# Two softmax products of an attention loop moved from VectorE to GpSimd, and the gate stage's scratch buffers halved

## The chip, the cores and the metric

The kernel runs as one program on all 8 NeuronCores of one Trainium2 chip, without any exchange between the cores. Each core works on half of one of four sequences. The metric is the device time of the slowest core in microseconds (us). Each core has five engines that run side by side and meet only in semaphores: TensorE (PE in the profile), VectorE (DVE), ScalarE (ACT), GpSimd (POOL) and SyncE (SP). DMAs are issued from the queues of SP, ACT and POOL.

## The reference

A layer of gated attention with bounded memory slots (ABC), then a mixture of low-rank maps, each added to its input and put through a layer norm. What matters here is the softmax in the middle of the attention and the gate behind it:

```python
z = cumlogsumexp(s); g = exp(z_prev - z); p = exp(s - z)
hk = hk * g_t + k_t * p_t;   ok = einsum('bhk,bhkm->bhm', q_t, hk)
pv = softmax(ok)                      # over M = 64 slots
hv = hv * g_t + p_t * v_t;   ov = einsum('bhm,bhmv->bhv', pv_t, hv)
g = x @ Wg
o = ov * rsqrt(mean(ov**2) + EPS) * g_norm_weight
o = o * (g * sigmoid(g));    x = layernorm(x + o @ Wo)
...                                    # mixture of 8 low-rank maps, second layer norm
```

There are 16 heads of 64 (keys, slots) and 128 (values), a model width of 2048 and 2048 positions in a sequence.

## The kernel before

A core first runs over 1024 positions that lie ahead of its own to get the recurrent states. Then it handles its own 1024 positions in two halves of 512, each of 4 chunks of 128 positions (NHC = 4). A half consists of stages: projections S, K, V and Q, the attention loop, the gate stage, the output product with Wo, a layer norm, and the mixture.

**The attention loop.** One turn is a chunk and a group of 4 heads (GH = 4), so a half has NIT = 16 turns, and the kernel has 32. The turns are pipelined by hand in the order of this loop, and every engine executes its own instructions in that order:

```python
for it in range(NIT + 1):
    if it < NIT:
        p_front(it)
    if 0 <= it - 1 < NIT:
        p_back(it - 1)
    if it < NIT:
        p_np(it)
        p_pv(it)
```

- `p_front` transposes keys, queries and e = exp(s) on TensorE; ScalarE copies them to `kqfm` and `efm`; TensorE multiplies them into FB[0], ScalarE copies this to `arw`, and GpSimd applies the causal mask (`abf`).
- `p_np` adds up numerator and denominator in a PSUM bank, FB[2] or FB[3].
- `p_pv` turns these into the weights. ScalarE makes `rbuf` = 1/denominator as exp(-ln), VectorE `okb` = numerator times `rbuf`, ScalarE `ebuf` = exp(`okb`); VectorE then sums `ebuf` per head into `sm4` (shown as sm), takes the reciprocal, multiplies `ebuf` by `rbuf` in place, and multiplies that by `sm4` into the bf16 tile `cbf`.
- `p_back` transposes `cbf` on TensorE (bank TBK[1], shown as tb); ScalarE copies it to `cfm`; TensorE multiplies with `efm` into FB[4], ScalarE copies this to `wrw`, GpSimd masks it (`wbf`), and TensorE makes the output and the update of the states, which VectorE adds to `s1f`, `psf` and `s2f` (each in float32).

**The gate stage** has two passes (vh = 0, 1) for the halves of the value columns. A pass first squares the 4 chunks of the attention's output `ovh` on ScalarE into a scratch tile `obs`, sums each on VectorE into `msq`, and takes square root and reciprocal once for all four. Then, for each chunk c: `g_proj(c)` multiplies with Wg on TensorE (32 products of 128x512), `g_evac(c)` copies the result on VectorE into `gsc`, and `g_gate(c)` takes Silu of it on ScalarE into `sgs`, multiplies `ovh` by `msq` and then by the norm weight on GpSimd into `obs`, multiplies `obs` by `sgs` on VectorE into the bf16 tile `otb`, and transposes `otb` on TensorE into `ofm`. TensorE's order in a pass is g_proj(0), g_proj(1), transposes of chunk 0, g_proj(2), transposes of chunk 1, and so on. `obs`, `sgs` and `otb` exist twice each, one for even and one for odd chunks. A pass ends in a barrier before the next begins.

**Waits.** A helper records each operation. On VectorE and ScalarE, and for operations recorded by `gop` on GpSimd, each instruction waits for its own engine's semaphore as well (the previous instruction's completion) besides the waits it names. Each wait is an instruction of its own (line 53), and `P.wait` leaves a wait out when that engine has already waited for the same or a later count of that semaphore:

```python
if n <= 0 or self.hw[eng].get(sem, 0) >= n:
    return
```

SBUF is handed out by a small allocator (`Arena`), which gives a new buffer the tokens of what was freed there to wait for.

Of the kernel before, what the change touches and what calls it, by code (L numbers as in the profile page):

```python
# [8 lines left out]
F32 = mybir.dt.float32  # L9
BF16 = mybir.dt.bfloat16  # L10
# [152 lines left out]
def build_program(cfg):  # L163
# [37 lines left out]
    with ctx:  # L201
# [65 lines left out]
        def vop(fn, waits=()):  # L267
            P.waits("vector", waits)
            P.wait("vector", ("VE", P.sems["VE"].n))
            return P.inc("vector", "VE", _eager(fn))  # L270

        def sop(fn, waits=()):
            P.waits("scalar", waits)
            P.wait("scalar", ("SC", P.sems["SC"].n))
            return P.inc("scalar", "SC", _eager(fn))
# [365 lines left out]
        for half in range(2):  # L641
# [155 lines left out]
            tok_cC = [None] * NIT  # L797
            tok_tc = [None] * NIT
            ex_prev = [None]

            def scp(out_ap, in_ap, waits=()):
                return sop(lambda s, o=out_ap, i=in_ap: s.copy(o, i), waits=waits)
# [86 lines left out]
            def p_pv(it):  # L889
                NPB = FB[2] if it % 2 == 0 else FB[3]  # L890
                cbf = cbfb[it % 2]
                lnp = sop(lambda s: s.activation(
                    rbuf.ap(0, 128, 0, GH * M), NPB[0:128, GH * M:2 * GH * M],
                    AF.Ln, bias=0.0, scale=1.0),
                    waits=[tok_mtN[it]] + rbuf.birth)
                vop(lambda v: v.memset(rbuf.h[0:1, 0:1], 0)) if False else None
                sop(lambda s: s.activation(
                    rbuf.ap(0, 128, 0, GH * M), rbuf.ap(0, 128, 0, GH * M),
                    AF.Exp, bias=0.0, scale=-1.0), waits=[lnp])
                ok = vop(lambda v: v.tensor_tensor(  # L900
                    okb.ap(0, 128, 0, GH * M), NPB[0:128, 0:GH * M],
                    rbuf.ap(0, 128, 0, GH * M), ALU.mult),
                    waits=[ex_prev[0], P.cur("SC")] + okb.birth)
                bset(NPB, ok)
                ex = sop(lambda s: s.activation(
                    ebuf.ap(0, 128, 0, GH * M), okb.ap(0, 128, 0, GH * M),
                    AF.Exp, bias=0.0, scale=1.0),
                    waits=[P.cur("VE")] + ebuf.birth)
                ex_prev[0] = ex
                vop(lambda v: v.tensor_reduce(  # L910
                    sm4.ap(0, 128, 0, GH),
                    ebuf.ap3(0, 128, 0, [[M, GH], [1, M]]), AX.X, ALU.add),
                    waits=[ex] + sm4.birth)
                vop(lambda v: v.reciprocal(sm4.ap(0, 128, 0, GH),
                                           sm4.ap(0, 128, 0, GH)))
                vop(lambda v: v.tensor_tensor(
                    ebuf.ap(0, 128, 0, GH * M), ebuf.ap(0, 128, 0, GH * M),
                    rbuf.ap(0, 128, 0, GH * M), ALU.mult))
                tok_cC[it] = vop(lambda v, cb=cbf: v.tensor_tensor(
                    cb.ap(0, 128, 0, GH * M), ebuf.ap(0, 128, 0, GH * M),  # L920
                    sm4.ap3(0, 128, 0, [[1, GH], [0, M]]), ALU.mult),
                    waits=([tok_tc[it - 2]] if it >= 2 else []) + cbf.birth)

            def p_back(it):
                c, g = divmod(it, NG)
# [135 lines left out]
            ofm = AR.alloc("ofm", [128, VDC * TH], BF16)  # L1061
            gsc2 = [AR.alloc("gsc", [128, GV], F32) for _ in range(2)]
            gsc2_free = [None, None]
            sgs2 = [AR.alloc("sgs", [128, GV], F32) for _ in range(2)]
            obs2 = [AR.alloc("obs", [128, GV], F32) for _ in range(2)]
            otb2 = [AR.alloc("otb", [128, GV], BF16) for _ in range(2)]
            otb_free2 = [None, None]
            sgs_free2 = [None, None]
            obs_free2 = [None, None]
            msq = AR.alloc("msq", [128, NHC * HH], F32)  # L1070
            ofm_tok = [None] * NHC
            wg_pre[1] = load_w("wgb2", wg, D, VD, col0=GV, ncols=GV)
# [1 line left out]
            for vh in range(2):  # L1074
                if vh == 1:
                    wo_pre[0] = load_w("wob2", wo, VD, D, col0=0, ncols=D2)
                wgb2, twg2 = wg_pre[vh]
                sq = None
                for c in range(NHC):
                    obs = obs2[c % 2]  # L1080
                    sq = sop(lambda s, c=c, vh=vh, obs=obs: s.activation(
                        obs.ap(0, 128, 0, GV),
                        ov_ap(c, vh * GV, GV), AF.Square,
                        bias=0.0, scale=1.0),
                        waits=bPAT + [obs_free2[c % 2]] + obs.birth)
                    obs_free2[c % 2] = vop(
                        lambda v, c=c, obs=obs: v.tensor_reduce(
                            msq.ap(0, 128, c * HH, HH),
                            obs.ap3(0, 128, 0, [[DV, HH], [1, DV]]),
                            AX.X, ALU.add),  # L1090
                        waits=[sq] + msq.birth)
                si = sop(lambda s: s.activation(msq.ap(0, 128, 0, NHC * HH),
                                                msq.ap(0, 128, 0, NHC * HH),
# [37 lines left out]

                def g_gate(c, vh):
                    gsc = gsc2[c % 2]
                    sgs = sgs2[c % 2]
                    obs = obs2[c % 2]
                    otb = otb2[c % 2]
                    sg = None
                    for g in range((GV + 511) // 512):
                        cn = min(512, GV - g * 512)
                        sg = sop(lambda s, g=g, cn=cn, sgs=sgs, gsc=gsc:  # L1140
                                 s.activation(
                            sgs.ap(0, 128, g * 512, cn),
                            gsc.ap(0, 128, g * 512, cn),
                            AF.Silu, bias=0.0, scale=1.0),
                            waits=[gv_tok[c][g], sgs_free2[c % 2]] + sgs.birth)
                    gsc2_free[c % 2] = sg
                    gop(lambda g, c=c, vh=vh, obs=obs: g.tensor_tensor(
                        obs.ap(0, 128, 0, GV),
                        ov_ap(c, vh * GV, GV),
                        msq.ap3(0, 128, c * HH, [[1, HH], [0, DV]]),  # L1150
                        ALU.mult), waits=[iv, obs_free2[c % 2]] + obs.birth)
                    o2 = gop(lambda g, obs=obs: g.tensor_tensor(
                        obs.ap(0, 128, 0, GV), obs.ap(0, 128, 0, GV),
                        gnw_sb.ap3(0, 128, 0, [[0, HH], [1, DV]]),
                        ALU.mult), waits=[t_gnw])
                    o3 = vop(lambda v, obs=obs, sgs=sgs, otb=otb:
                             v.tensor_tensor(
                        otb.ap(0, 128, 0, GV), obs.ap(0, 128, 0, GV),
                        sgs.ap(0, 128, 0, GV), ALU.mult),
                        waits=[sg, o2, otb_free2[c % 2]] + otb.birth)  # L1160
                    sgs_free2[c % 2] = o3
                    obs_free2[c % 2] = o3
                    for j0 in range(0, HH, 4):
                        nj = min(4, HH - j0)
                        bnk = TBK[j0 // 4 % 2]
                        mt = None
                        for j in range(nj):
                            mt = mm(bnk[0:128, j * 128:(j + 1) * 128],
                                    otb.ap(0, 128, (j0 + j) * DV, DV),
                                    idb_sb.h[0:128, 0:128],  # L1170
                                    start=(j == 0), stop=(j == nj - 1),
                                    waits=[o3, t_idb, bfree(bnk)] if j == 0 else (),
                                    inc=(j == nj - 1), tp=True)
                        evt = vop(lambda v, b=bnk, nj=nj, c=c, j0=j0, vh=vh:
                                  v.tensor_copy(
                                      ofm.ap3(0, 128,
                                              (vh * HH + j0) * TH + c * 128,
                                              [[TH, nj], [1, 128]]),
                                      b[0:128, 0:nj * 128]),
                                  waits=[mt] + ofm.birth)  # L1180
                        bset(bnk, evt)
                        ofm_tok[c] = evt
                    return P.cur("MM")

                for c in range(NHC + 1):
                    if c < NHC:
                        g_proj(c)
                    if c - 1 >= 0:
                        otb_free2[(c - 1) % 2] = g_gate(c - 1, vh)
                    if c < NHC:  # L1190
                        g_evac(c)
                bPAT = phase_barrier()
                AR.freebuf(wgb2, toks=bPAT)
                AR.freebuf(ovhh[vh], toks=bPAT)

            for b in (msq, otb2[0], otb2[1], obs2[0], obs2[1], sgs2[0],
                      sgs2[1], gsc2[0], gsc2[1]):
                AR.freebuf(b, toks=bPAT)
            AR.freebuf(xmf, toks=bPAT)

# [462 lines left out]
```

How the kernel before makes its waits and increments, by code:

```python
    def wait(self, eng, tok):  # L43
        if tok is None:
            return
        sem, n = tok
        if sem in self.ONESHOT and n > 0:
            n = self.sems[sem].n
        if n <= 0 or self.hw[eng].get(sem, 0) >= n:
            return
        self.hw[eng][sem] = n
        h = self.sems[sem].h
        self.streams[eng].append(lambda e, h=h, n=n: e.wait_ge(h, n))
        self.ninst[eng] += 1
# [9 lines left out]
    def inc(self, eng, sem, fn, dn=1):  # L64
        s = self.sems[sem]
        s.n += dn
        h = s.h
        self.streams[eng].append(lambda e, fn=fn, h=h, dn=dn: fn(e).then_inc(h, dn))
        self.ninst[eng] += 1
        return (sem, s.n)
```

## Time and profile before

| what | us |
|---|---|
| median of 3 runs (1890.65 to 1899.34) | 1892.87 |
| the profiled execution: its own time | 1893.43 |
| the profiled execution: span of its slowest core (core 5) | 1891.9 |
| spans of the 8 cores | 1876.2 to 1891.9 |
| TensorE busy on core 5 | 1306.0 |
| VectorE busy | 544.5 |
| ScalarE busy | 412.6 |
| GpSimd busy | 234.4 |

The profile is one execution, read on its slowest core; times in it are counted from the first instruction. The own time of the execution is 1.5 us more than the span. The attention loops lie at about 576 to 786 and 1324 to 1534, the gate stages at about 787 to 866 and 1535 to 1614. PE rows show matrix products, whose overlap lets their mean duration exceed their spacing; some of their records can be missing. Idle time in square brackets ahead of an instruction is followed by what ended it.

### The profile page before, as it was taken

Reading aid. Unit: us, or ns where it says so; the run is one execution under the profiler, and the core shown is the slowest. Engines: PE = TensorE matmul, PEld = TensorE weight load, DVE = VectorE, ACT = ScalarE, POOL = GpSimd, SP = SyncE. Lnnn points to the kernel's source line nnn. Section 1 sums busy time; section 2 is a strip of 40 time slices with the busy share of each in tenths; the row PEclk is TensorE's granted clock in tenths of the full one; section 3 lists DMA queues with packets and bytes.
Section 4 is the critical chain, followed back from the end, with each engine's and each line's share of the span. In section 5 each row is a group of like instructions: output and inputs, shape, how many; then the busy total and the mean of one; then the engine's idle time right before and its main releaser. Section 6 shows DMA issues by size and latency. Waiting matters only on the chain.

```text
span 1891.9 us, 18782 instructions; the slowest of 8 cores (1876.2 to 1891.9 us)
## 1 busy us (share of the span) xinstructions
PE 1306.0 (69%) x6800; PEld 643.1 (34%) x6800; DVE 544.5 (29%) x886; ACT 412.6 (22%) x568; POOL 234.4 (12%) x220
## 2 busy tenths in 40 slices
PE   2449898978995554588585757979555568758662
PEld 0114444434443333344242323424333334324231
DVE  2012323242001222354431272000222245352145
ACT  0000000001113444421110122102444432120013
POOL 2100000000002111251100001100211145110000
PEclk9769999988995555689887768979555579979776
DMA  9950010002405000277975149980500046893502
GB/s 175 178 97 23 26 42 23 23 25 81 73 1 90 1 1 1 42 113 156 219 117 89 16 74 225 172 137 1 90 1 1 1 78 101 172 179 72 89 1 89
DMA packets 61515, 146.25 MB, mean 77 GB/s; under 512 B 7536, under 2 KB 12016, under 8 KB 56048
## 3 DMA queue, kind: packets, MB, share of 16 engines
q0 software_dynamic: 54800, 102.90, 35.1%
q1 hardware_dynamic: 5472, 33.76, 5.4%
q10 hardware_dynamic: 1152, 8.39, 1.1%
q8 instruction: 55, 0.90, 0.2%
q14 instruction: 36, 0.29, 0.1%
HBM read 237.45 MB, written 8.39 MB: 130 GB/s over the span
## 4 chain that ended last, share of the span: by engine, by line
PE 47%; DMA 18%; DVE 15%; ACT 8%; issue 6%; POOL 4%; DVEq 1%; ACTq 0%; POOLq 0%
PE fb L245 45%; DMA wvb<-wv 6%; DMA wob<-wo 4%; DMA wkb<-wk 3%; DMA w1b<-w 3%; PE tb L245 2%; POOL wbf L265 2%; DMA wsb<-ws 1%; ACT rbuf L265 1%; DVE x1bufs L265 1%; DVE msq L265 1%; DVE st L265 1%; ACT wrw L265 1%; ACT cfm L265 1%; DVE sm L265 1%
## 5 line engine op out<-in xcount | busy, mean ns | idle before, releaser
L245 PE MATMUL fb<-w1b,x2fm 128*128 128x512 bf16 x512 | 130.5, 417 | 34.5 <-DMA w1b<-w 34.5
L245 PE MATMUL fb<-wvb,xpf 128*128 128x512 bf16 x512 | 119.1, 393 | 31.8 <-DMA wvb<-wv 31.8
L245 PE MATMUL fb<-wob,ofm 128*128 128x512 bf16 x512 | 118.0, 394 | 19.4 <-DMA wob<-wo 19.4
L245 PE MATMUL fb<-wvb,xmf 128*128 128x512 bf16 x512 | 117.2, 392 | 13.9 <-DMA wvb<-wv 13.9
L245 PE MATMUL fb<-wgb,xmf 128*128 128x512 bf16 x512 | 122.0, 401 | 0.0
L265 DVE TENSOR_TENSOR okb<-fb,rbuf 128x256 f32<-128x256 f32 x32 | 13.6, 424 | 310.2 <-ACT rbuf L265 168.9
L245 PE MATMUL fb<-wsb,xpf 128*128 128x512 bf16 x256 | 70.0, 435 | 32.8 <-DMA wsb<-ws 19.5
L245 PEld LDWEIGHTS fb<-w1b,x2fm 128*128 128x128 bf16 x512 | 52.1, 104 | 105.4 <-issue 57.0
L265 DVE TENSOR_TENSOR s1f<-s1f,fb 64x256 f32<-64x256 f32 (+1 forms) x48 | 24.1, 502 | 209.0 <-PE fb L245 207.3
L245 PEld LDWEIGHTS fb<-wvb,xpf 128*128 128x128 bf16 x512 | 50.6, 100 | 97.5 <-issue 42.8
L245 PEld LDWEIGHTS fb<-wob,ofm 128*128 128x128 bf16 x512 | 51.4, 101 | 85.3 <-issue 30.0
L245 PE MATMUL fb<-idf,strip 128*128 128x128 f32 x256 | 42.1, 302 | 55.1 <-DVE xmf L265 28.2
L245 PEld LDWEIGHTS fb<-wvb,xmf 128*128 128x128 bf16 x512 | 50.9, 100 | 79.9 <-issue 23.0
L245 PE MATMUL fb<-wsb,xmf 128*128 128x512 bf16 x256 | 68.6, 435 | 8.5 <-DVE xmf L265 8.5
L245 PEld LDWEIGHTS fb<-wgb,xmf 128*128 128x128 bf16 x512 | 52.1, 103 | 64.9 <-issue 12.4
L245 PE MATMUL fb<-wkb,xpf 128*128 128x512 bf16 x256 | 62.0, 398 | 14.2 <-DMA wkb<-wk 14.2
L265 POOL TENSOR_TENSOR abf<-arw,lmb 128x512 bf16<-128x512 bf16 x32 | 36.8, 1151 | 273.7 <-ACT arw L265 273.7
L265 ACT ACTIVATE scrf<-x1bufs 128x1024 f32<-128x1024 f32 (+1 forms) x24 | 32.2, 1342 | 163.8 <-DVE x1bufs L265 163.8
L245 PE MATMUL fb<-utb,vxwf 128*128 128x512 bf16 x128 | 50.7, 583 | 24.0 <-DVE x1bufs L265 21.5
L265 ACT ACTIVATE scrb<-scrf 128x1024 bf16<-128x1024 f32 x16 | 16.9, 1057 | 230.3 <-DVE scrf L265 230.3
L265 ACT ACTIVATE echk<-fb,pb 128x512 bf16<-128x512 f32 x16 | 11.0, 688 | 251.9 <-DVE fb L265 251.9
L265 DVE TENSOR_SCALAR fb<-fb 128x512 f32<-128x512 f32 x32 | 22.4, 699 | 142.6 <-PE fb L245 141.8
(149 smaller groups left out, 1897.7 us busy)
## 6 DMA issues: line engine op xcount, KB each, us to landing
strip<-x_main SPq DMA_DIRECT2D x24, 1024.0 KB, 10.1
wvb<-wv POOLq DMA_DIRECT2D x16, 1024.0 KB, 34.7
wgb<-wg POOLq DMA_DIRECT2D x16, 1024.0 KB, 19.6
wob<-wo POOLq DMA_DIRECT2D x16, 1024.0 KB, 21.2
w1b<-w POOLq DMA_DIRECT2D x16, 1024.0 KB, 23.6
strip<-x_pre SPq DMA_DIRECT2D x8, 1024.0 KB, 8.2
wqb<-wq POOLq DMA_DIRECT2D x8, 1024.0 KB, 32.0
y<-x1bufs ACTq DMA_DIRECT2D x8, 1024.0 KB, 4.8
```

What stands on the lines that cost most here:

```text
L245: t.matmul(o, l, r, start=a, stop=b, is_transpose=(True if tpp else None)))
L265: return lambda e, n=name, a=a, k=k: getattr(e, n)(*a, **k)
```

## The change

In `p_pv`, the product of `ebuf` with `rbuf` and the product into `cbf` are recorded for GpSimd in place of VectorE. The first waits for the exponential, for the second activation into `rbuf` and for the sum `sm`; the second for the reciprocal. New waits guard the buffers: the logarithm into `rbuf` waits for the previous turn's first product, and the exponential into `ebuf` and the sum into `sm4` wait for the previous turn's second product. In the gate stage, `obs`, `sgs` and `otb` exist once each in place of twice, with the waits that this asks for.

```diff
                 lnp = sop(lambda s: s.activation(
                     rbuf.ap(0, 128, 0, GH * M), NPB[0:128, GH * M:2 * GH * M],
                     AF.Ln, bias=0.0, scale=1.0),
-                    waits=[tok_mtN[it]] + rbuf.birth)
-                vop(lambda v: v.memset(rbuf.h[0:1, 0:1], 0)) if False else None
-                sop(lambda s: s.activation(
+                    waits=[tok_mtN[it], e2_prev[0]] + rbuf.birth)
+                rex = sop(lambda s: s.activation(
...
                 ex = sop(lambda s: s.activation(
                     ebuf.ap(0, 128, 0, GH * M), okb.ap(0, 128, 0, GH * M),
                     AF.Exp, bias=0.0, scale=1.0),
-                    waits=[P.cur("VE")] + ebuf.birth)
+                    waits=[P.cur("VE"), cC_prev[0]] + ebuf.birth)
                 ex_prev[0] = ex
-                vop(lambda v: v.tensor_reduce(
+                sm = vop(lambda v: v.tensor_reduce(
                     sm4.ap(0, 128, 0, GH),
                     ebuf.ap3(0, 128, 0, [[M, GH], [1, M]]), AX.X, ALU.add),
-                    waits=[ex] + sm4.birth)
-                vop(lambda v: v.reciprocal(sm4.ap(0, 128, 0, GH),
-                                           sm4.ap(0, 128, 0, GH)))
-                vop(lambda v: v.tensor_tensor(
+                    waits=[ex, cC_prev[0]] + sm4.birth)
+                rc = vop(lambda v: v.reciprocal(sm4.ap(0, 128, 0, GH),
+                                                sm4.ap(0, 128, 0, GH)))
+                e2_prev[0] = gop(lambda g: g.tensor_tensor(
                     ebuf.ap(0, 128, 0, GH * M), ebuf.ap(0, 128, 0, GH * M),
-                    rbuf.ap(0, 128, 0, GH * M), ALU.mult))
-                tok_cC[it] = vop(lambda v, cb=cbf: v.tensor_tensor(
+                    rbuf.ap(0, 128, 0, GH * M), ALU.mult),
+                    waits=[ex, rex, sm])
+                tok_cC[it] = gop(lambda g, cb=cbf: g.tensor_tensor(
                     cb.ap(0, 128, 0, GH * M), ebuf.ap(0, 128, 0, GH * M),
                     sm4.ap3(0, 128, 0, [[1, GH], [0, M]]), ALU.mult),
-                    waits=([tok_tc[it - 2]] if it >= 2 else []) + cbf.birth)
+                    waits=[rc] + ([tok_tc[it - 2]] if it >= 2 else [])
+                    + cbf.birth)
+                cC_prev[0] = tok_cC[it]
...
-            sgs2 = [AR.alloc("sgs", [128, GV], F32) for _ in range(2)]
-            obs2 = [AR.alloc("obs", [128, GV], F32) for _ in range(2)]
-            otb2 = [AR.alloc("otb", [128, GV], BF16) for _ in range(2)]
-            otb_free2 = [None, None]
-            sgs_free2 = [None, None]
-            obs_free2 = [None, None]
+            sgs = AR.alloc("sgs", [128, GV], F32)
+            obs = AR.alloc("obs", [128, GV], F32)
+            otb = AR.alloc("otb", [128, GV], BF16)
+            otb_free = None
+            sgs_free = [None]
...
-                        waits=bPAT + [obs_free2[c % 2]] + obs.birth)
+                        waits=bPAT + [obs_free] + obs.birth)
...
-                        ALU.mult), waits=[iv, obs_free2[c % 2]] + obs.birth)
+                        ALU.mult), waits=[iv, sgs_free[0]] + obs.birth)
...
-                        waits=[sg, o2, otb_free2[c % 2]] + otb.birth)
-                    sgs_free2[c % 2] = o3
-                    obs_free2[c % 2] = o3
+                        waits=[sg, o2, otb_free] + otb.birth)
+                    sgs_free[0] = o3
```

## Rows read from the trace of the kernel before

**Rows 1.** The page's head: its span.
```profile
span 1891.9 us, 18782 instructions; the slowest of 8 cores (1876.2 to 1891.9 us)
```

**Rows 2.** Windows: stretch, length, busy us (instructions) of PE, PEld, DVE, ACT, POOL, PEclk, DMA, GB/s.
```profile
586.00:786.00 200.00, 105.05 (x781) 71.12 (x780) 52.08 (x123) 90.81 (x145) 34.44 (x30) 0.51 0.09 15
...
860.00:865.00 5.00, 0.38 (x5) 0.41 (x6) 3.14 (x5) 1.26 (x2) 0.00 (x0) 0.70 0.00 0
```

**Rows 3.** Timeline of one turn of the attention loop: start us, busy us, instruction.
```profile
643.79 0.39 ACT L265 ACTIVATE rbuf<-fb 128x256 f32<-128x256 f32 x1 [1.94 <-PE fb L245]
...
644.27 0.42 ACT L265 ACTIVATE rbuf<-rbuf 128x256 f32<-128x256 f32 x1
...
644.86 0.42 DVE L265 TENSOR_TENSOR okb<-fb,rbuf 128x256 f32<-128x256 f32 x1 [0.63 <-ACT rbuf L265]
645.43 0.42 ACT L265 ACTIVATE ebuf<-okb 128x256 f32<-128x256 f32 x1 [0.74 <-DVE okb L265]
...
646.02 0.42 DVE L265 TENSOR_REDUCE sm<-ebuf 128x4 f32<-128x256 f32 x1 [0.74 <-ACT ebuf L265]
646.54 0.18 DVE L265 RECIPROCAL sm<-sm 128x4 f32<-128x4 f32 x1
646.82 0.42 DVE L265 TENSOR_TENSOR ebuf<-ebuf,rbuf 128x256 f32<-128x256 f32 x1
...
647.35 0.42 DVE L265 TENSOR_TENSOR cbf<-ebuf,sm 128x256 bf16<-128x256 f32 x1
647.81 0.59 ACT L265 CAST arw<-fb 128x512 bf16<-128x512 f32 x1 [0.20 <-PE fb L245]
...
648.03 0.60 PE L245 MATMUL tb<-idb,cbf 128*64 128x128 bf16 x4 [0.36 <-DVE cbf L265]
648.54 1.15 POOL L265 TENSOR_TENSOR abf<-arw,lmb 128x512 bf16<-128x512 bf16 x1 [8.15 <-ACT arw L265]
648.78 0.58 ACT L265 COPY cfm<-tb 64x512 bf16<-64x512 bf16 x1 [0.38 <-PE tb L245]
...
649.50 0.58 PE L245 MATMUL fb<-cfm,efm 64*128 64x128 bf16 x4 [0.87 <-ACT cfm L265]
```

**Rows 4.** Timeline of the gate stage's first pass, half 0, other engines than TensorE.
```profile
788.83 5.19 DVE L265 TENSOR_REDUCE msq<-obs 128x8 f32<-128x1024 f32 x4 [4.62 <-ACT obs L265]
790.20 1.06 ACT L265 ACTIVATE obs<-ovh 128x1024 f32<-128x1024 f32 x1 [0.46 <-DVE msq L265]
...
796.34 1.89 POOL L265 TENSOR_TENSOR obs<-ovh,msq 128x1024 f32<-128x1024 f32 x1 [5.26 <-DVE msq L265]
...
798.38 2.34 POOL L265 TENSOR_TENSOR obs<-obs,gnw 128x1024 f32<-128x1024 f32 x1
...
800.86 1.89 POOL L265 TENSOR_TENSOR obs<-ovh,msq 128x1024 f32<-128x1024 f32 x1
800.89 2.95 DVE L265 TENSOR_TENSOR otb<-obs,sgs 128x1024 bf16<-128x1024 f32 x1 [3.11 <-POOL obs L265]
...
808.30 3.35 DVE L265 TENSOR_TENSOR otb<-obs,sgs 128x1024 bf16<-128x1024 f32 x1 [1.02 <-POOL obs L265]
811.86 1.90 POOL L265 TENSOR_TENSOR obs<-ovh,msq 128x1024 f32<-128x1024 f32 x1 [1.29 <-DVE otb L265]
...
817.10 1.23 DVE L265 TENSOR_TENSOR otb<-obs,sgs 128x1024 bf16<-128x1024 f32 x1 [1.02 <-ACT sgs L265]
```

**Rows 5.** Timeline of TensorE after chunk 0's gate, first and second pass.
```profile
803.98 1.01 PE L245 MATMUL tb<-idb,otb 128*128 128x128 bf16 x8 [7.33 <-DVE otb L265]
...
804.79 8.35 PE L245 MATMUL fb<-wgb,xmf 128*128 128x512 bf16 x32
...
844.42 0.61 PE L245 MATMUL tb<-idb,otb 128*128 128x128 bf16 x8 [1.38 <-DVE otb L265]
...
844.87 7.07 PE L245 MATMUL fb<-wgb,xmf 128*128 128x512 bf16 x32
```

**Rows 6.** Groups by line of GpSimd, whole span: count, busy us, mean ns.
```profile
L182 POOL MEMSET const-float32-0.0<- 128x1 f32 x1 | 0.1, 98 | 0.5 <-issue 0.5
```

More of the change, by code:

```diff
@@ L799, in build_program @@
             ex_prev = [None]
+            e2_prev = [None]
+            cC_prev = [None]
             def scp(out_ap, in_ap, waits=()):
@@ L1078, in build_program @@
                 sq = None
+                obs_free = None
                 for c in range(NHC):
-                    obs = obs2[c % 2]
-                    sq = sop(lambda s, c=c, vh=vh, obs=obs: s.activation(
+                    sq = sop(lambda s, c=c, vh=vh: s.activation(
                         obs.ap(0, 128, 0, GV),
@@ L1084, in build_program @@
                         bias=0.0, scale=1.0),
-                        waits=bPAT + [obs_free2[c % 2]] + obs.birth)
[L1086 to L1090, printed above, removed]
+                        waits=bPAT + [obs_free] + obs.birth)
+                    obs_free = vop(lambda v, c=c: v.tensor_reduce(
+                        msq.ap(0, 128, c * HH, HH),
+                        obs.ap3(0, 128, 0, [[DV, HH], [1, DV]]), AX.X, ALU.add),
                         waits=[sq] + msq.birth)
@@ L1133, in g_gate @@
                     gsc = gsc2[c % 2]
-                    sgs = sgs2[c % 2]
-                    obs = obs2[c % 2]
-                    otb = otb2[c % 2]
                     sg = None
@@ L1139, in g_gate @@
                         cn = min(512, GV - g * 512)
-                        sg = sop(lambda s, g=g, cn=cn, sgs=sgs, gsc=gsc:
-                                 s.activation(
+                        sg = sop(lambda s, g=g, cn=cn: s.activation(
                             sgs.ap(0, 128, g * 512, cn),
@@ L1144, in g_gate @@
                             AF.Silu, bias=0.0, scale=1.0),
-                            waits=[gv_tok[c][g], sgs_free2[c % 2]] + sgs.birth)
+                            waits=[gv_tok[c][g], sgs_free[0]] + sgs.birth)
                     gsc2_free[c % 2] = sg
-                    gop(lambda g, c=c, vh=vh, obs=obs: g.tensor_tensor(
+                    gop(lambda g, c=c, vh=vh: g.tensor_tensor(
                         obs.ap(0, 128, 0, GV),
@@ L1150, in g_gate @@
                         msq.ap3(0, 128, c * HH, [[1, HH], [0, DV]]),
-                        ALU.mult), waits=[iv, obs_free2[c % 2]] + obs.birth)
-                    o2 = gop(lambda g, obs=obs: g.tensor_tensor(
+                        ALU.mult), waits=[iv, sgs_free[0]] + obs.birth)
+                    o2 = gop(lambda g: g.tensor_tensor(
                         obs.ap(0, 128, 0, GV), obs.ap(0, 128, 0, GV),
@@ L1155, in g_gate @@
                         ALU.mult), waits=[t_gnw])
-                    o3 = vop(lambda v, obs=obs, sgs=sgs, otb=otb:
-                             v.tensor_tensor(
+                    o3 = vop(lambda v: v.tensor_tensor(
                         otb.ap(0, 128, 0, GV), obs.ap(0, 128, 0, GV),
                         sgs.ap(0, 128, 0, GV), ALU.mult),
-                        waits=[sg, o2, otb_free2[c % 2]] + otb.birth)
-                    sgs_free2[c % 2] = o3
-                    obs_free2[c % 2] = o3
+                        waits=[sg, o2, otb_free] + otb.birth)
+                    sgs_free[0] = o3
                     for j0 in range(0, HH, 4):
@@ L1188, in build_program @@
                     if c - 1 >= 0:
-                        otb_free2[(c - 1) % 2] = g_gate(c - 1, vh)
+                        otb_free = g_gate(c - 1, vh)
                     if c < NHC:
@@ L1194, in build_program @@
                 AR.freebuf(ovhh[vh], toks=bPAT)
-            for b in (msq, otb2[0], otb2[1], obs2[0], obs2[1], sgs2[0],
-                      sgs2[1], gsc2[0], gsc2[1]):
+            for b in (msq, otb, obs, sgs, gsc2[0], gsc2[1]):
                 AR.freebuf(b, toks=bPAT)
```

## The prediction

> **What bounds the kernel now.** I read the page's head first [rows 1], then the chain of work that ended last, then a timeline of one turn of the attention loop [rows 3] and of a pass of the gate stage [rows 4, 5], and at the end windows over the stages [rows 2]. No engine is the bound where the change lands. In the 200 us of the attention loop no engine is busy for more than 105 us, and the DMA engines do nothing much (0.09) [rows 2]. The reader is to see in [rows 3] that the loop is one serial thread: each instruction of it begins 0.1 to 0.3 us after the one before it ends, on another engine or the same. Numerator and denominator, logarithm, exponential, `okb`, `ebuf`, sum, reciprocal, product, product, transposes of `cbf`, copy to `cfm`, product into FB[4], mask, output, and then TensorE goes on to the next turn's numerator, which stands behind all this in its queue. So every 0.1 us added to this thread is paid 32 times. In the gate stage the reader is to see that TensorE stands idle before the first transposes of each pass (7.33 and 1.38 us) and that this idle time ends with `otb` of chunk 0 [rows 5]. From the squares to `otb` of chunk 0 it is one thread too. After it TensorE runs g_proj(2) and g_proj(3) and is the thread itself.
>
> **Waits, priced.** Each wait is an instruction, so the gap ahead of an operation tells its price. On ScalarE the gap with one wait is 644.27 - 644.18 = 0.09 us and with two 645.43 - 645.28 = 0.15: 0.06 for a wait. On VectorE 0.10 with one (646.54 - 646.44) and 0.17 with two (646.02 - 645.85): 0.07. On TensorE 0.14 with one (649.50 - 649.36) and 0.26 with two (648.03 - 647.77): 0.12 [rows 3]. On GpSimd 0.15 with one (798.38 - 798.23) and 0.21 with two, after VectorE (811.86 - 811.65) [rows 4].
>
> **Attention loop, what goes and what comes.** From the end of the sum (646.44) to the start of the transposes (648.03) it is 1.59 us now: gap 0.10, reciprocal 0.18, gap 0.10, product 0.42, gap 0.11, product 0.42, gap 0.26 [rows 3]. After the change the first product needs the sum but not the reciprocal, which runs beside it on VectorE at no cost (0.10 + 0.18 us after the sum; its cover is the GpSimd product, over 0.5 us long). If that cover fails, it costs at most what is left of the 0.28 us. The new thread is: gap to GpSimd with two waits 0.21, first product, gap 0.15, second product, gap to TensorE 0.26.
>
> The trace has no GpSimd product of 256 elements. The nearest are two of 1024 float32 elements, 2.34 us with two plain operands and 1.89 with one operand repeated along the row [rows 4], and the mask of 512 bf16 elements, 1.15 [rows 3]. By size alone the first product (two plain operands) is 2.34/4 = 0.585 and the second (`sm4` repeated along the row, like `msq`) 1.89/4 = 0.47. That is the low end, as size alone leaves no fixed part. A fixed part is bounded by the memset of one column, 0.10 [rows 6]: 0.10 + 2.24/4 = 0.66 for either is the high end, as the second may not have the faster rate with bf16 out and rows of 64. The far bound, 1.15 each, is that of twice the elements and is left out, since 2.34 against 1.15 shows time going with size. I take 0.64 and 0.56, nearer the high end, since some fixed part is likely. The new stretch is 0.21 + 0.64 + 0.15 + 0.56 + 0.26 = 1.82, which is 0.23 more than 1.59.
>
> By the Trainium skill (GPSIMD Engine Reference, section Elementwise, side-by-side cycle accounting) a two-input product of 2048 float32 elements takes 4497 ns on GpSimd. An estimate from that page's figure and the trace's 2.34 us for 1024 makes the fixed part 0.19 and a product of 256 elements 0.73 us; with 0.73 for both the stretch would be 0.49 longer than now in place of 0.23, and the total below about 8 us higher. No row here shows 2048 elements.
>
> **Waits that are added on the thread.** The logarithm waits for the previous first product and the exponential into `ebuf` for the previous second one. Both are long done, but each is an instruction behind a wait that resolves late: 2 x 0.06 on ScalarE. The sum waits for it too: 0.07 on VectorE. A fourth is not in the diff. TensorE used to wait on VectorE's semaphore for `cbf`, and this covered the wait of the product into FB[4] for its bank (freed by VectorE's `s2f` addition). Now `cbf` is counted by GpSimd's semaphore, so `P.wait` no longer drops the bank's wait: 0.12 on TensorE between `cfm` and that product. Together 0.31 a turn. Queued behind them are only the instructions of the same thread. The mask `abf` of the next turn now stands behind the second product on GpSimd. That product ends at about 646.51 + 0.21 + 0.64 + 0.15 + 0.56 = 648.07 on the old turn's clock, while `abf` can't start before 648.54, when `arw` is copied [rows 3], so it isn't delayed; above 0.5 us more it would be.
>
> Sum for the loop: 0.23 + 0.31 = 0.54 a turn, x 32 = 17.3 us. With the low products (0.585, 0.47) it is 0.39 and 12.6 us, with the high ones (0.66, 0.66) 0.66 and 21 us. If the added waits cost nothing because they are taken off ahead of time, the low end is 0.085 a turn, 2.7 us. TensorE's granted clock is 0.51 in the loop, its level of 1.2 GHz [rows 2]; it can't fall further through longer gaps.
>
> **Gate stage, squares.** With two `obs` tiles the four sums into `msq` follow each other: 788.83 + 5.19 = 794.02 is the end [rows 4]. With one, square c+1 waits for sum c. Square 1.06, gap 0.17, sum 1.22, gap 0.15 (790.20 - 790.05 [rows 4]) make a period of 2.60. The first sum ends at 790.05, the fourth at 790.05 + 3 x 2.60 = 797.85: 3.8 us later. All of it lies on the thread to `otb` of chunk 0 (`msq`, two GpSimd products, `otb`).
>
> **Gate stage, what comes back.** `otb` of chunk 0 takes 2.95 us, that of chunk 2, when GpSimd is idle, 1.23. GpSimd begins chunk 1's product at 800.86, 0.03 before `otb` at 800.89; 1.86 of waiting and 1.09 of work make 2.95 [rows 4]. With one `obs`, GpSimd's chunk 1 waits for `otb` of chunk 0, so the two can't meet: 1.72 us less. Net 3.8 - 1.7 = 2.1 us later for the first transposes of a pass, in 4 passes: 8.4 us. The rule behind this is in the Trainium skill (SBUF, section Who interferes with whom): a VectorE instruction with two SBUF inputs and a GpSimd instruction that reads SBUF hold a shared port pair one at a time. The trace agrees (2.95 against 1.23). The same rule lets the reciprocal and the reduction pass beside GpSimd, as assumed above; no row here shows that.
>
> The rest of a pass stays hidden. Chunk 1 on GpSimd now begins after `otb` of chunk 0 and takes 0.21 + 1.89 + 0.15 + 2.34, then `otb` 0.2 + 1.23, 6.0 us in all; TensorE is busy for at least 7.07 with g_proj(2) before it asks for it [rows 5]. Should it take 1 us more than I think, nothing happens yet. Chunks 2 and 3 have the same period and as much room.
>
> TensorE's idle time in second passes grows from 1.38 to about 3.5 us. After 1.38 us the next 32 products took 7.07; after 7.33 they took 8.35 and the transposes 0.4 more [rows 5]. So the price is between 0 and 1.7 us in each of two second passes. I take 0.8 each, 1.6 together. First passes pay this already.
>
> Nothing swallows the delay: between the gate stage and the load of the second half of Wo, which the output product waits for, the DMA engines stand idle (0.00 [rows 2]), so that load is issued later by what the gate stage is late. The allocator puts all weight buffers where they were, worked through on paper with the smaller set, so no load gets other tokens.
>
> **Sum.** 17.3 + 8.4 + 1.6 = 27.3 us on the profiled execution's 1893.43 (span 1891.9 and 1.5 around it [rows 1]), which is 0.6 above the median of 1892.87. I forecast 1920. What a measurement of this kernel can tell from no change is about 0.5%, 9.5 us.
>
> **The rivals.**
> - *Only size counts and waits are free.* The wait instructions resolve early and GpSimd has no fixed part: 2.7 + 8.4 = 11 us, 1904. For it: the waits' tokens are old. Against: they stand behind late ones in the same queue. Chance 0.12; together with a smaller gate loss part of it falls within 0.5%.
> - *GpSimd's small products are dear.* Fixed part of 0.2 us or more (the estimate above), or rows of 64 slow: 0.8 each, a stretch 0.63 longer, 0.94 a turn with the waits, 30 us + 10 = 40, 1933. For it: no row of a short product. Chance 0.17.
> - *The squares hide and the loop's waits hide* while the GpSimd products cost by size: 2.7 less 4 x 1.72, 1889, or 12.6 less the same if only the squares hide, 1899; no measurable change. Against it: the idle time before the first transposes ends with `otb`, in both passes. Chance 0.06.
> - *Unblocking wins.* If what TensorE waits for were `otb` in every chunk, and the squares were hidden, lifting the blocking would give back 1.72 in a first chunk and 3.35 - 1.23 = 2.12 in the next, 3.8 a pass, 15 us in 4 passes, and with the loop at its low end of 2.7 us 1881: faster. It decides from the point where `otb` of chunk 1 ends after g_proj(2). Against it: 808.30 + 3.35 = 811.65 lies before 804.79 + 8.35 = 813.14 [rows 4, 5]. Chance 0.03.
> - *As forecast*: 0.62.
>
> Range 1905 to 1932: the lower end takes in most of the first rival, the upper the high products, the full clock price and part of the second. Slower by over 0.5%: 0.87; within 0.5%: 0.10; faster: 0.03.
>
> **What would show it.** A turn's stretch from `sm` to the transposes of 1.8 us (1.6 now), GpSimd products of 0.64 and 0.56, a gap of about 0.26 ahead of FB[4]'s product, turns 0.5 us longer; sums into `msq` 2.6 us apart; all `otb` at 1.23; TensorE idle 2 us longer before a pass's first transposes; the second passes' first 32 products between 7.1 and 8.4 us. The prediction is wrong if GpSimd products are far from 0.6, or if the four added waits don't show in the gaps.

## The result and the profile after

The changed kernel takes 1928.0 us (median of 9 runs; the kernel before, run beside it, 1896.4 over 10): a ratio of 1.0167, 95% interval 1.0151 to 1.0183, or some 31.6 us more. Some executions of the runs below were disturbed, and the ratios leave them out. The forecast was 1920 in a range of 1905 to 1932.

From the page of the changed kernel:

```profile
span 1924.4 us, 19006 instructions; the slowest of 8 cores (1910.9 to 1924.4 us)
...
PE 1312.9 (68%) x6800; PEld 645.8 (34%) x6800; DVE 505.1 (26%) x822; ACT 412.5 (21%) x568; POOL 271.9 (14%) x284
```

VectorE has 64 instructions fewer and GpSimd 64 more; VectorE's busy time falls by 39 us (the moved products, and otb rows that no longer stand blocked). None of that shortens anything, as no engine was the bound.

One turn of the loop in the changed kernel, timeline, against [rows 3]:

```profile
647.69 0.42 DVE L265 TENSOR_TENSOR okb<-fb,rbuf 128x256 f32<-128x256 f32 x1 [0.68 <-ACT rbuf L265]
648.32 0.42 ACT L265 ACTIVATE ebuf<-okb 128x256 f32<-128x256 f32 x1 [0.80 <-DVE okb L265]
...
648.98 0.42 DVE L265 TENSOR_REDUCE sm<-ebuf 128x4 f32<-128x256 f32 x1 [0.86 <-ACT ebuf L265]
649.50 0.18 DVE L265 RECIPROCAL sm<-sm 128x4 f32<-128x4 f32 x1
649.60 0.72 POOL L265 TENSOR_TENSOR ebuf<-ebuf,rbuf 128x256 f32<-128x256 f32 x1 [6.43 <-DVE sm L265]
...
650.47 0.61 POOL L265 TENSOR_TENSOR cbf<-ebuf,sm 128x256 bf16<-128x256 f32 x1
...
651.34 0.61 PE L245 MATMUL tb<-idb,cbf 128*64 128x128 bf16 x4 [0.78 <-ACT arw L265]
...
652.09 0.58 ACT L265 COPY cfm<-tb 64x512 bf16<-64x512 bf16 x1 [0.80 <-PE tb L245]
...
652.92 0.58 PE L245 MATMUL fb<-cfm,efm 64*128 64x128 bf16 x4 [0.98 <-ACT cfm L265]
...
658.98 0.39 ACT L265 ACTIVATE rbuf<-fb 128x256 f32<-128x256 f32 x1 [2.00 <-PE fb L245]
...
660.68 0.42 ACT L265 ACTIVATE ebuf<-okb 128x256 f32<-128x256 f32 x1 [0.80 <-DVE okb L265]
```

The reader is to see the products at 0.72 and 0.61 us, 1.94 us from the end of the sum (649.40) to the transposes (651.34) where it was 1.59, and four gaps that have grown: 0.21 ahead of the exponential (0.15 before), 0.24 ahead of the sum (0.17), 0.25 ahead of the product into FB[4] (0.14), and the one ahead of the logarithm, 0.06 more by the idle time in its row (2.00 for 1.94). A turn takes 660.68 - 648.32 = 12.36 us. The releaser named in one row misleads: the transposes' row names `arw`, where [rows 3] name `cbf`, but they begin 0.26 us after `cbf` ends at 651.08, the same gap as before.

The first pass of the gate stage, half 0, timeline (VectorE and GpSimd), against [rows 4]:

```profile
801.17 1.22 DVE L265 TENSOR_REDUCE msq<-obs 128x8 f32<-128x1024 f32 x1 [1.38 <-ACT obs L265]
...
803.76 1.22 DVE L265 TENSOR_REDUCE msq<-obs 128x8 f32<-128x1024 f32 x1 [1.38 <-ACT obs L265]
...
806.36 1.22 DVE L265 TENSOR_REDUCE msq<-obs 128x8 f32<-128x1024 f32 x1 [1.38 <-ACT obs L265]
...
814.46 1.22 DVE L265 TENSOR_TENSOR otb<-obs,sgs 128x1024 bf16<-128x1024 f32 x1 [3.11 <-POOL obs L265]
...
815.89 1.90 POOL L265 TENSOR_TENSOR obs<-ovh,msq 128x1024 f32<-128x1024 f32 x1 [1.60 <-DVE otb L265]
```

The sums stand 2.6 us apart, `otb` takes 1.22, and GpSimd waits for it. TensorE after chunk 0's gate, timeline, first pass and second, against [rows 5]:

```profile
815.83 1.01 PE L245 MATMUL tb<-idb,otb 128*128 128x128 bf16 x8 [8.88 <-DVE otb L265]
...
816.64 9.38 PE L245 MATMUL fb<-wgb,xmf 128*128 128x512 bf16 x32
...
859.10 1.01 PE L245 MATMUL tb<-idb,otb 128*128 128x128 bf16 x8 [4.49 <-DVE otb L265]
...
859.90 8.23 PE L245 MATMUL fb<-wgb,xmf 128*128 128x512 bf16 x32
```

The first 32 products after the gap take 9.38 and 8.23 us where they took 8.35 and 7.07.

This table is worked out from such rows. "Turn" is the spacing of the rows of `ebuf` on ScalarE. "Loop" is from the first of them to the end of the last copy to `psb`, in half 0 of the slowest core. "Gate" runs from there to the end of the last transposes of `otb`, both halves added, as the mean of the 8 cores.

| kernel | turn | loop, one half | gate, both halves |
|---|---|---|---|
| before | 11.73 | 206.2 | 156.5 |
| changed | 12.35 | 215.6 | 169.3 |
| e1, loop only | 12.36 | 215.7 | 159.7 |
| e2, gate only | 11.72 | 206.1 | 171.8 |
| e3, waits early | 12.06 | 210.9 | 168.1 |
| e4, scratch tiles for squares | 12.35 | 215.6 | 157.7 |
| e5, filled gap | 12.35 | 215.7 | 165.0 |
| e6, product beside the sum | 11.44 | 200.9 | 162.7 |
| e7, scratch, loop of before | 11.72 | 206.1 | 158.8 |
| e8, e6 and e7 | 11.44 | 200.9 | 152.0 |
| e9, before again | 11.72 | 206.1 | 160.6 |
| e10, changed again | 12.35 | 215.6 | 172.6 |
| e11, as e7 | 11.73 | 206.1 | 153.2 |

The loop is 9.5 us longer in half 0 and 10.0 in half 1, and the gate 12.8, together 32.3. The spans of the 8 cores grow by 32.7 us on average and the measured time by 31.6, so this is the whole loss.

Where the table differs between kernels with the same gate code (156.5 and 160.6 for the kernel before, 169.3 and 172.6 for the changed one, 156.5 and 159.7 for e1), it shows stretches of a lower granted clock, of which e9 to e11 tell. The ratios below are each against the kernel before in runs beside them, which had a median of 1904.8 us for e1 to e4 and of 1907.3 for e5 to e8, so a few us of difference between a ratio and the 1.0167 above are not to be read.

### The profile page after: what moved, and what is told of

It is laid out like the page before. It is cut to its first block, busy times and chain, and to the rows that moved or that the text cites. A ratio compares the mean times of both kernels' runs of the same rounds, so it can differ in the third digit from the quotient of the medians.

```text
span 1924.4 us, 19006 instructions; the slowest of 8 cores (1910.9 to 1924.4 us)
## 1 busy us (share of the span) xinstructions
PE 1312.9 (68%) x6800; PEld 645.8 (34%) x6800; DVE 505.1 (26%) x822; ACT 412.5 (21%) x568; POOL 271.9 (14%) x284
## 4 chain that ended last, share of the span: by engine, by line
PE 50%; DMA 15%; DVE 13%; ACT 10%; issue 6%; POOL 4%; DVEq 1%; ACTq 1%; POOLq 0%
PE fb L245 47%; DMA wvb<-wv 6%; DMA wob<-wo 4%; DMA w1b<-w 3%; PE tb L245 2%; POOL wbf L265 2%; ACT kqfm L265 1%; DMA wsb<-ws 1%; ACT rbuf L265 1%; DVE x1bufs L265 1%; DMA wkb<-wk 1%; DVE msq L265 1%; DVE st L265 1%; DVE xmf L265 1%; ACT wrw L265 1%
## 5 line engine op out<-in xcount | busy, mean ns | idle before, releaser
L245 PE MATMUL fb<-wgb,xmf 128*128 128x512 bf16 x512 | 126.3, 411 | 0.0
L245 PE MATMUL fb<-kqfm 64*128 64x128 bf16 x128 | 18.2, 292 | 68.1 <-ACT kqfm L265 68.1
L233 POOL DMA_DIRECT2D wqb<-wq x8 | 6.0, 760 | 395.7 <-ACT eh L265 395.7
```

The costliest lines, as they stand in the source:

```text
L233: lambda e, o=out_ap, i=in_ap: e.dma_start(out=o, in_=i), 16)
L245: t.matmul(o, l, r, start=a, stop=b, is_transpose=(True if tpp else None)))
```

## The experiments

**The two halves of the change.** e1 is the changed loop with the gate stage of before, e2 the changed gate stage with the loop of before.

> The loop's half of the change with the gate stage of before. Theory: a turn grows from 11.72 to 12.36 us (longer GpSimd products and four added waits), 32 x 0.64 = 20.5 us, so about 1.011 of before, and the gate stage stays as it was. Rival, that the gate stage carries most of the loss: under 12 us, below 1.007.

Measured: 1.0112 (1.0053 to 1.0171), a turn of 12.36.

> The gate stage's half of the change with the loop of before. Theory: 8.4 us from the serial squares less the lifted blocking, plus some 6 us of TensorE at its lower level after longer idle time, 14 us, 1.0075 of before. Rival, that the clock rows belong to something else in the changed loop: 8.4 us, 1.0045, and the second passes' first 32 products at 7.07.

Measured: 1.0057 (1.0023 to 1.0092), the loop untouched. The interval holds both the theory's 1.0075 and the rival's 1.0045, so the rows decide: behind the gap, the second passes of the slowest core ran their 32 products in 9.57 and 9.39 us, so these long rows don't need the changed loop. The two ratios add up to the whole.

**The price of the waits.** e3 puts three of the four added waits ahead of the wait that resolves late. The fourth, ahead of the exponential, goes: the logarithm now waits for the previous turn's second product in place of its first, and this covers it.

```diff
-                    waits=[tok_mtN[it], e2_prev[0]] + rbuf.birth)
+                    waits=[cC_prev[0], tok_mtN[it]] + rbuf.birth)
...
-                    waits=[P.cur("VE"), cC_prev[0]] + ebuf.birth)
+                    waits=[P.cur("VE")] + ebuf.birth)
...
-                    waits=[ex, cC_prev[0]] + sm4.birth)
+                    waits=[cC_prev[0], ex] + sm4.birth)
...
-                            waits=([tok_cC[it], t_idb, bfree(TBK[1])]
+                            waits=([bfree(FB[4]), tok_cC[it], t_idb, bfree(TBK[1])]
```

> The changed kernel with the four added waits of a turn put ahead of the wait that resolves late. Theory, each wait behind a late one costs its 0.06 to 0.12 us: a turn 12.36 - 0.30 = 12.06 us, about 9.6 us less than the changed kernel, 1.0115 of before. Rival, that waits on old tokens are free: turn 12.36, nothing gained.

Timeline of e3, ScalarE and TensorE:

```profile
646.56 0.42 ACT L265 ACTIVATE ebuf<-okb 128x256 f32<-128x256 f32 x1 [0.75 <-DVE okb L265]
...
650.25 0.58 ACT L265 COPY cfm<-tb 64x512 bf16<-64x512 bf16 x1 [0.72 <-PE tb L245]
650.97 0.58 PE L245 MATMUL fb<-cfm,efm 64*128 64x128 bf16 x4 [0.87 <-ACT cfm L265]
...
658.62 0.42 ACT L265 ACTIVATE ebuf<-okb 128x256 f32<-128x256 f32 x1 [0.75 <-DVE okb L265]
```

The gap ahead of FB[4]'s product is back at 0.14 us and the turn is 658.62 - 646.56 = 12.06, 0.30 less. The ratio is 1.0111 (1.0065 to 1.0157), the loop 2 x 4.7 us shorter. The waits were on old tokens and still cost 0.30 us a turn, for they were executed behind the late one. The rival, that they are free, is out. Of the 0.30, the 0.06 of the exponential were won by leaving its wait out and not by moving it.

**The gate without serial squares.** e4 gives the squares two scratch tiles of their own (`sqs2`) and leaves `obs`, `sgs` and `otb` single.

```diff
+            sqs2 = [AR.alloc("sqs", [128, GV], F32) for _ in range(2)]
...
-                    sq = sop(lambda s, c=c, vh=vh: s.activation(
-                        obs.ap(0, 128, 0, GV),
+                    sqs = sqs2[c % 2]
+                    sq = sop(lambda s, c=c, vh=vh, sqs=sqs: s.activation(
+                        sqs.ap(0, 128, 0, GV),
...
-                        waits=bPAT + [obs_free] + obs.birth)
+                        waits=bPAT + [sqs_free[c % 2]] + sqs.birth)
```

> The changed kernel with two scratch tiles of their own for the squares, while obs, sgs and otb stay single in the gate. Theory: sums 1.3 us apart again and otb of 1.23 us, so a pass is 1.7 us shorter than before and TensorE's idle time in second passes falls to nothing: the loop's 20.5 less 7, some 13.5 us over before, 1.007. Rival, that the single obs in the gate is what costs (GpSimd's next chunk waits for otb): still near 1.0167.

Measured: 1.0101 (1.0057 to 1.0145). The gate loses the change's loss (157.7 for 169.3), so single buffers in the gate itself are not what costs. It falls short of the 149.6 that the theory asks for (156.5 less 4 x 1.72). Many of its g_proj took 8.57 us (see e9 to e11), and the 32 products behind the first pass's gap took 9.4 us in half 0 on all cores, where they took 8.35 in the kernel before, although the gap was shorter (5.3 us for 7.3).

**The clock after idle time.** e5 adds products of no use to the changed kernel, ahead of chunk 0's transposes, where TensorE would stand idle.

```diff
+                    if c == 1:
+                        for i in range(32 if vh == 0 else 14):
+                            mm(FB[4][0:128, 0:512], xslc(0)(i % KC),
+                               wgb2.ap(0, 128, (i % KC) * GV, 512),
+                               start=True, stop=True,
+                               waits=[bfree(FB[4])] if i == 0 else ())
                     if c - 1 >= 0:
                         otb_free = g_gate(c - 1, vh)
```

> The changed kernel with added products of no use (32 in a first pass, 14 in a second, 128x512 into the bank FB[4] that this stage leaves free) ahead of chunk 0's transposes, where TensorE stands idle. Theory, TensorE falls to its lower level after long idle time: with the gap filled g_proj(2) takes 7.07 us in every pass and the transposes 0.61, some 9 us less than the changed kernel, 1.012 of before. Rival, that g_proj(2) is long for another reason (a bank or a port): it stays at 8.2 to 9.4.

Timeline of e5, TensorE of core 0, first and second pass of half 0:

```profile
813.83 0.61 PE L245 MATMUL tb<-idb,otb 128*128 128x128 bf16 x8 [1.96 <-DVE otb L265]
814.27 7.07 PE L245 MATMUL fb<-wgb,xmf 128*128 128x512 bf16 x32
...
854.43 0.61 PE L245 MATMUL tb<-idb,otb 128*128 128x128 bf16 x8
854.88 7.07 PE L245 MATMUL fb<-wgb,xmf 128*128 128x512 bf16 x32
```

Windows of the changed kernel (core 5) during and after the first 5 us behind the gap, and of e5 (core 0) in the same place:

```profile
816.00:820.00 4.00, 4.00 (x16) 1.85 (x15) 2.23 (x4) 1.26 (x2) 3.86 (x2) 0.50 1.09 170
822.00:826.00 4.00, 4.00 (x22) 1.88 (x21) 0.00 (x0) 0.00 (x0) 3.86 (x2) 1.00 1.08 195
```

```profile
814.00:822.00 8.00, 8.00 (x50) 4.05 (x48) 3.72 (x6) 1.26 (x2) 6.11 (x4) 1.00 1.08 179
```

Behind the gap the granted clock is 0.50 (1.2 GHz) and then 1.00 (2.4 GHz) in the changed kernel, and 1.00 throughout in e5. With the gap filled the 32 products take 7.07 us in both passes, and on six cores the two halves' gates take 80.5 and 80.9 us where the changed kernel's take 84.6 and 84.7 (means of the 8 cores), 8 us less. The ratio is 1.0090 (1.0052 to 1.0128). So the long rows were the granted clock after idle time. The kernel before pays for it too, in its first passes: from the start of chunk 0's transposes to the end of the next 32 products its four passes take 33.6 us together (mean of the 8 cores), where 4 x 7.51 is the time at full clock. That is 3.5 us, so without the clock its gate would be 153.0, and 153.0 + 8.4 for the later transposes is e5's 161.4. On cores 4 and 5 the halves took 90 and 85 us: on core 5 all g_proj of 32 products in half 0, and in the second pass of half 1, took 8.57; of these below.

**A use of GpSimd that pays.** e6 takes the kernel before and moves only the first product, into a tile of its own, so that it can start with the sum and not after it. The second stays on VectorE.

```diff
+                e2 = gop(lambda g: g.tensor_tensor(
+                    prbuf.ap(0, 128, 0, GH * M), ebuf.ap(0, 128, 0, GH * M),
+                    rbuf.ap(0, 128, 0, GH * M), ALU.mult),
+                    waits=[cC_prev[0], ex, rex] + prbuf.birth)
...
-                vop(lambda v: v.tensor_tensor(
-                    ebuf.ap(0, 128, 0, GH * M), ebuf.ap(0, 128, 0, GH * M),
-                    rbuf.ap(0, 128, 0, GH * M), ALU.mult))
                 tok_cC[it] = vop(lambda v, cb=cbf: v.tensor_tensor(
-                    cb.ap(0, 128, 0, GH * M), ebuf.ap(0, 128, 0, GH * M),
+                    cb.ap(0, 128, 0, GH * M), prbuf.ap(0, 128, 0, GH * M),
                     sm4.ap3(0, 128, 0, [[1, GH], [0, M]]), ALU.mult),
-                    waits=([tok_tc[it - 2]] if it >= 2 else []) + cbf.birth)
+                    waits=([tok_tc[it - 2]] if it >= 2 else []) + [e2]
+                    + cbf.birth)
```

> The kernel before with only the first product on GpSimd, into a tile of its own, so that it runs beside the sum on VectorE; the second product stays on VectorE, and the new waits stand ahead of the late ones. Theory: from ebuf to the transposes 1.74 us in place of 2.18, but ScalarE's queue (arw) then holds cfm until 0.29 us before where it was: a turn 11.43, 9 us less than before, 0.995. Rival, that a GpSimd product must cost the thread wherever it stands: a turn of 11.9 or more, 1.003.

Timeline of a turn of e6:

```profile
642.50 0.42 DVE L265 TENSOR_REDUCE sm<-ebuf 128x4 f32<-128x256 f32 x1 [0.73 <-ACT ebuf L265]
642.53 0.73 POOL L265 TENSOR_TENSOR prbuf<-ebuf,rbuf 128x256 f32<-128x256 f32 x1 [5.66 <-ACT ebuf L265]
...
643.43 0.43 DVE L265 TENSOR_TENSOR cbf<-prbuf,sm 128x256 bf16<-128x256 f32 x1 [0.23 <-POOL prbuf L265]
...
643.57 0.58 PE L245 MATMUL fb<-kqfm 64*128 64x128 bf16 x4 [2.02 <-ACT kqfm L265]
644.23 0.60 PE L245 MATMUL tb<-idb,cbf 128*64 128x128 bf16 x4
644.29 0.59 ACT L265 CAST arw<-fb 128x512 bf16<-128x512 f32 x1 [0.21 <-PE fb L245]
...
644.98 0.58 ACT L265 COPY cfm<-tb 64x512 bf16<-64x512 bf16 x1
```

The reader is to see the sum and the product side by side, `cbf` beginning 0.51 us after the sum ends (0.91 in [rows 3]), and then the next bound: the transposes stand behind another product in TensorE's queue (643.57, four of them), and `cfm` starts 0.10 us after `arw` ends at 644.88, with no idle time named. The turn is 11.44, 0.29 less than before, as expected. The two halves of the loop give 5.3 and 4.8 us. The ratio is 0.9967 (0.9942 to 0.9991), some 6 us: in the trace part of the loop's gain goes in the gate, 162.7 us with the code of before, where the 8.57 us rows are found again.

**The shorter gate on the loop of before, and both together.**

> The kernel before with the gate of e4 (single obs, sgs and otb, two scratch tiles for the squares). Theory: 1.72 us less in each of 4 passes and no longer idle time, 7 us, 0.996 of before, where TensorE's granted clock is the same. Rival, that single buffers cost by themselves: over 1.000.

Measured: 0.9997 (0.9979 to 1.0014): no change.

> The loop of e6 and the gate of e7 together. Theory: their gains add, 9 and 7 us, 0.9915 of before. Rival: a shorter loop or gate only meets a load that is not there yet, and the sum stays under 10 us.

Measured: 0.9902 (0.9867 to 0.9936), the best of all versions, some 18 us faster than the kernel before, with gates of 152.0 us for 156.5 and a turn of 11.44. The rival is out. But the ratio rests on three executions, and e6 and e7, measured alone, give 6 and 1 us; the stages of the traces give 10 and 4.5. Of the 18 us, some 15 are thus seen in the loop and the gate.

**Where e7's gain went.** In many rows of e4, e5, e6 and e7, g_proj took 8.57 us, a value that the first traces of the two kernels don't show on any core. I took it that TensorE, used more fully, is held back. Three more traces were made side by side.

> The kernel before once more, for its trace on the same chip as the two runs beside it. Question: does TensorE run 32 products in 8.57 us (a granted clock between its levels) in the gate stage of this kernel too? Theory, those stretches come with fuller use of TensorE: fewer of them over the 8 cores than in the gate with scratch tiles, gate stages of 78 us. Rival, they belong to the chip alone: as many in each of the three runs.

> The changed kernel once more on this chip. Gate stages of 84.7 us as in its first trace, a turn of 12.35 us. By the theory, with longer idle time it has few or no stretches of 8.57; by the rival, as many as the others.

> The gate with single obs, sgs and otb and scratch tiles for the squares, once more on this chip. By the theory more stretches of 8.57 than the kernel before and gate stages of 78 to 80 us; by the rival as many as in the other two, and where there are none 74.5.

Of the rows with 32 products of g_proj, the 8 cores show 8.57 or 8.58 us 16 times in e9, 11 times in e10 and 12 times in e11. Timeline of e9, the kernel before, core 4, second pass, and below it a window over part of it (the columns of [rows 2]):

```profile
854.53 0.70 PE L245 MATMUL tb<-idb,otb 128*128 128x128 bf16 x8
855.06 8.57 PE L245 MATMUL fb<-wgb,xmf 128*128 128x512 bf16 x32
```

```profile
852.00:866.00 14.00, 12.07 (x58) 5.51 (x57) 6.24 (x10) 1.29 (x3) 4.33 (x3) 0.81 0.47 84
```

The granted clock is 0.81 where it is 1.00 in the 7.07 rows. So the shorter gate isn't needed for these stretches: the kernel before has them too, and in this gate more of them. More than that the three traces don't tell of my theory. By the clock records of the traces, a core spent 93 us of the whole execution at a granted clock of 0.81 in e9, 125 in e10 and 156 in e11 (means of the 8 cores). The kernel with the shorter gate has most, but the changed kernel, whose gate is the longest, comes next. The first traces of the kernel before and of the changed one have none, e7 has 242 and e8, with the same gate, 31. Whether a fuller TensorE brings more of them stays open.

Between e9 and e11, made side by side, the gate is 160.6 against 153.2 us, 7.4 less, with 16 and 12 such rows. The 10 halves of e11 (of 16) without them take 73.0 to 76.2 us, the 16 of the first trace of the kernel before, which has none, 77.7 to 79.2. In e9 the halves with them take 83.5 to 83.7, some 5.4 us more. So the shorter gate is in the traces, and e7's measured time, over other executions, doesn't show it. Its 7 us are of the size of what such stretches add or take on the slowest core: the fastest core of e11 has a span of 1852.4 us and its slowest 1902.1. That this swallowed e7's gain is argued, not shown. A rival is that a later stage only waits longer for a load; e8 speaks against it: from the gate of half 0 to the first `ebuf` of half 1 it takes 458.8 us (means of the 8 cores), for 460.0 in the first trace of the kernel before, and e7, with the same gate, 466.8.

## Why the prediction was right, step by step

- **One serial thread in the loop; no engine is the bound.** Right. Every change of the thread by e1, e3 and e6 came back in the turn. The mask `abf` is not delayed either: it starts 0.14 us after `arw` ends, as before (651.43).
- **The four added waits, 0.31 us a turn.** Right: 0.30, by the gaps and by e3, the hidden one on TensorE among them (0.25 for 0.14).
- **GpSimd's products, 0.64 and 0.56, stretch 0.23 longer.** Under-sized: 0.72 and 0.61, and 0.35 longer. This is the term that was most off in the loop, 0.12 a turn, 3.8 us. Both products lie above the straight share of the 1024-element rows, the first beyond the high end of 0.66: the memset of one column is no bound for the fixed part of a product. The estimate from the Trainium skill (GPSIMD Engine Reference, section Elementwise, side-by-side cycle accounting), whose figure is for an addition, was 0.73 (0.72 when worked out again), and the trace agrees for the product with two plain operands (0.72), not for the one with the repeated operand (0.61). The row of 2.34 us that the prediction took for two plain operands has one, `gnw`, that is a row of 128 read 8 times; no run tells what difference that makes.
- **The reciprocal is free beside the product.** Right: 0.18 us as before, and the product starts on time. It agrees with the Trainium skill (SBUF, section Who interferes with whom) that a VectorE instruction with one SBUF input, outside of its 2-port modes, does not contend: in e6 a sum of 0.42 and a GpSimd product of 0.73 run at once.
- **Loop in all: 17.3.** Measured 19.5, over 15 spacings of each half and what follows its last `ebuf`. By the turn's 0.63, 32 turns would be 20.
- **Squares 3.8 later, blocking 1.7 back, 2.1 net a pass.** Right. From the end of the last `psb` copy to the first transposes it was 803.98 - 787.38 = 16.60 us and is 815.83 - 797.13 = 18.70; from the end of the first pass's last transposes to the second's first it was 17.31 and is 19.39.
- **The rest of a pass stays hidden.** Right: only the transposes of chunks 0 and 3 have idle time before them, as before. The 5.2 to 4.9 us ahead of chunk 3's is old.
- **TensorE's clock, 1.6, second passes only.** Under-sized and half wrong in its reasoning. "First passes pay this already" fails: they paid more (9.38 for 8.35, and 8.72 for 8.13 in half 1). Second passes of the slowest core paid 1.16 and 2.35 and 0.4 each for the transposes, the second of them more than the 1.7 that the prediction took as its bound, and their idle time was 4.49 and 3.31 us where it expected about 3.5. Over the 8 cores the gate lost 12.8, so the clock's part is 12.8 - 8.4 = 4.4 us. The rows say the same: from the start of chunk 0's transposes to the end of the next 32 products the two first passes together take 1.4 us more than before and the two second passes 3.0. So it isn't enough that a pass has had its gap, and the length of the gap doesn't give the price either; the last section has the rows.
- **Nothing swallows the delay.** Right: 19.5 + 12.8 is the whole of the measured 31.6.

The sum was 27.3 and the measurement 31.6. Both missing parts, some 2 us in the loop and some 3 us of clock in the gate, are sizes of terms that were there, but for the 1.4 us of the first passes, which the prediction put at nothing. Three of the rivals did not come: waits were not free, the squares did not hide, and GpSimd's blocking was not what TensorE waited for beyond chunk 0. The rival of dear small products came in part: its fixed part of about 0.2 us is there, its 0.8 us a product is not. Both errors went the same way, so neither hid the other.

## What to carry to other kernels

Where a loop is one serial thread through all engines, moving work off a lightly used engine gains nothing, and what counts is the latency of each step with its hand-over; work helps on another engine only if it can start earlier, beside the thread, as the product in a tile of its own did. A wait on a token long past costs its 0.06 to 0.12 us if it stands behind one that resolves late and nothing if it stands ahead, and moving a producer to another engine can bring back waits that its semaphore had covered. A scratch tile shared by two uses can serialize the first use while single buffering is harmless to the second: give the first its own.

## What the runs showed of the hardware that was not expected

- A GpSimd product of 128x256 float32 takes 0.72 us and one with a repeated operand and bf16 out 0.61, against 2.34 and 1.89 for 1024 elements, which leaves about 0.2 us that don't shrink with size (0.18 in each pair, taken as a straight line).
- TensorE's price for idle time does not go by the length of the gap. In second passes the 32 products behind it took 7.07 us after 1.4 us of it. After 3.0 to 5.0 us, in the gate with serial squares, they took 8.0 to 9.6 on many cores and 7.07 on others: in the changed kernel's own trace after 3.38 us on core 0 and 3.35 on core 6, but 9.42 after 3.31 on core 5, all in half 1. In first passes they took 8.35 after 7.33 us (before), 9.38 after 8.88 (changed), and 9.22 after only 5.59 (e11, core 0):

```profile
800.06 1.01 PE L245 MATMUL tb<-idb,otb 128*128 128x128 bf16 x8 [5.59 <-DVE otb L265]
800.87 9.22 PE L245 MATMUL fb<-wgb,xmf 128*128 128x512 bf16 x32
```

- Beside its two levels TensorE had stretches with a granted clock of 0.81, in which 32 products took 8.57 us, on some cores and in some executions of every kernel of the later sets, the kernel before too. They come on neighbouring cores together (0 and 1, 2 and 3, and so on) and not always on a whole die (cores 0 to 3, 4 to 7): from 834 to 870 us in e2 the granted clock is 0.81 on cores 0 and 1 and 0.89 to 0.91 on the other six, and in e9 cores 2 to 7 have such a stretch from about 810 us on and cores 0 and 1 none.
